# A PixArt block of 16 samples on one core: where the biases, the stacks and the maxima stand in hand-written plans

## The chip, the cores and the metric

The kernel runs on one core of a Trainium2 chip. The metric is the device time of one execution in microseconds; the median of three runs stands for the kernel. All times here are microseconds unless marked ns.

## The reference

16 samples, each with 256 tokens of 256 channels, all in fp32. For each sample, with `_ln` a layer norm without weights and 16 heads of 16 channels:

```
c_proj = silu(c) @ W_mod + b_mod       -> shift_a, scale_a, gate_a, shift_m, scale_m, gate_m
q, k, v = modulate(_ln(x), shift_a, scale_a) @ W_qkv + b_qkv
x = x + gate_a * (softmax(q k^T / 4) v @ W_proj + b_proj)            self attention
q_c = _ln(x) @ W_qc + b_qc;  k_c, v_c = _ln(context) @ W_kvc + b_kvc
x = x + softmax(q_c k_c^T / 4) v_c @ W_cproj + b_cproj               cross attention
x = x + gate_m * (gelu(modulate(_ln(x), shift_m, scale_m) @ W_mlp1 + b_mlp1) @ W_mlp2 + b_mlp2)
```

## The kernel before, in words

Names ending in x belong to self attention, in y to cross attention, m to the MLP, c to the context. Everything stays on the chip between stages of a sample; five engines each run one in-order program, tied by semaphores.

The work is a software pipeline over t from -1 to 18. Each t has a section A and a section B, each of 16 slots. In a slot of A, TensorE computes one head's scores of x(t) with queries on the partitions (the "scan", L637), of which VectorE takes the row maximum (L924), and one head's transposed scores of y(t-2) (L647), which ScalarE turns into P by an exponential (L778). In B the same is done with scans of y(t-1) and scores of x(t). There are two scan banks and two score banks in PSUM: slot s needs the reduction and the exponential of slot s-2.

Precision comes from splitting each fp32 operand into a high and a low part that TensorE takes at its rounded format. A query stack QS holds, per head pair and parity, 16 rows of high, 16 of high, 16 of low parts, and one row with the negated row maxima; a key stack KS holds high, low, high, and ones. ScalarE writes the high part of a projection (`projected`, L723, then semaphore `s_hi`), VectorE the low part (L840, then `s_lo`), and SyncE moves them into the stack with six transfers (L305), or for the queries of y, whose stack has only one buffer, six for each half (`q_y0`, `q_y1`, L317). The maxima are transposed on TensorE (L560), copied by ScalarE into MT (L751), and SyncE moves them into the stack's extra rows (`maxima`, L325): two transfers, one for each parity. TensorE waits for the stack before the first scan of a section, and for the maxima rows before slots 0 and 8 of the scores.

All other work is put between slots by plans: for each engine and section a list of (task, shift of t, slot), run in that order after the slot's own work (`run`, L270). SyncE and GpSimd have no slot work, so only the order counts for them. The tasks that matter here: `T_y` transposes the normed xn_y; `q_y` projects it; `norm_y` writes xn_y on VectorE (L825) with the inverse root of `root_y` from GpSimd (L397, L399); `x_bias`, `x1_bias` and `x2_bias` add a bias row to a residual on GpSimd (L441, L449, L458); `gate` multiplies the output weights by the gate (L434); `up0` to `up3`, `down0` and `down1` are the MLP; `pv_*` weights the values; `pt`, `pn`, `po` turn, norm and turn back its result. Projections and transposes go through two further PSUM banks in turn; a task waits until the one two places before it has been copied out (`take`, L511).

Of the kernel before, what the change touches and what calls it, by code (L numbers as in the profile page):

```python
# [4 lines left out]
fp32 = mybir.dt.float32  # L5
# [5 lines left out]
B, N, H, NH, MLP = 16, 256, 256, 16, 1024  # L11
HD = H // NH
# [11 lines left out]


SP_PLAN = {
    "A": [("gate_a", 0, 3), ("max_y1", -2, 3), ("gate_m", -3, 4), ("x_in", 2, 7), ("k_x", 1, 11), ("max_x0", 0, 12),
          ("q_y0", -1, 12), ("q_y1", -1, 13), ("q_x", 1, 15)],
    "B": [("c_in", 1, 0), ("max_x1", 0, 0), ("max_y0", -1, 1), ("k_y", 0, 4), ("out", -3, 15)],
}  # L30
PE_PLAN = {
    "A": [("up0a", -3, 0), ("up1a", -3, 0), ("up0b", -3, 0), ("up1b", -3, 0), ("pv_x3", -1, 1), ("max_y1", -2, 1),
          ("v_xa", 0, 2), ("v_xb", 0, 2), ("T_x", 1, 2), ("up2a", -3, 3), ("up2b", -3, 5), ("out_xa", -1, 5),
          ("out_xb", -1, 5), ("k_xa", 1, 7), ("k_xb", 1, 7), ("up3a", -3, 7), ("pv_y0", -2, 7), ("up3b", -3, 7),
          ("T_y", -1, 8), ("max_x0", 0, 9), ("pv_y1", -2, 9), ("q_ya", -1, 10), ("q_yb", -1, 10), ("q_xa", 1, 11),
          ("q_xb", 1, 12), ("pv_y2", -2, 15)],
    "B": [("pv_y3", -2, 1), ("max_x1", 0, 1), ("v_ya", -1, 1), ("v_yb", -1, 1), ("down0a", -3, 2), ("down0b", -3, 4),
          ("out_ya", -2, 4), ("out_yb", -2, 4), ("T_c", 0, 5), ("pv_x0", 0, 6), ("k_ya", 0, 7), ("k_yb", 0, 7),
          ("max_y0", -1, 9), ("pv_x1", 0, 9), ("T_m", -2, 11), ("down1a", -3, 11), ("down1b", -3, 13),
          ("pv_x2", 0, 15)],  # L40
}
ACT_PLAN = {
    "A": [("up0", -3, 0), ("up1", -3, 0), ("max_y1", -2, 1), ("v_x", 0, 2), ("T_x", 1, 2), ("up2", -3, 5),
          ("k_x", 1, 6), ("up3", -3, 7), ("T_y", -1, 7), ("q_y", -1, 10), ("max_x0", 0, 10), ("q_x", 1, 11)],
    "B": [("max_x1", 0, 0), ("v_y", -1, 0), ("T_c", 0, 5), ("k_y", 0, 7), ("max_y0", -1, 8), ("T_m", -2, 11)],
}
DVE_PLAN = {
    "A": [("pt_x1", -1, 0), ("stats_c", 0, 2), ("pn_x1", -1, 3), ("po_x1", -1, 3), ("out_x", -1, 5),
          ("stats_y", -1, 6), ("k_x", 1, 7), ("norm_y", -1, 7), ("T_y", -1, 8), ("pt_y0", -2, 10), ("q_y", -1, 11),
# [3 lines left out]
          ("stats_x", 2, 14)],  # L53
}
POOL_PLAN = {
    "A": [("norm_x", 1, 0), ("gate", -1, 2), ("T_x", 1, 3), ("root_y", -1, 7), ("x_bias", 0, 9), ("x2_bias", -3, 10)],
    "B": [("norm_c", 0, 0), ("norm_m", -2, 9), ("T_m", -2, 9), ("sum0", -3, 15), ("x1_bias", -1, 15),
          ("sum1", -3, 15)],
}
BANKED = {"up0", "up1", "up2", "up3", "max_x0", "max_x1", "max_y0", "max_y1", "out_x", "out_y", "T_c", "T_y", "T_x",  # L60
          "T_m", "k_x", "q_x", "k_y", "q_y", "v_x", "v_y", "down0", "down1"}
# [40 lines left out]
def build(nc, x, ctx_in, cond, bias, rows_in, bv_rows, wm1, wm2, wqk, wvx, wqc, wkvc, wo, wup, wdown, out):  # L102
# [3 lines left out]
    def wait(eng, sem, value):  # L106
        if value > 0:
            eng.wait_ge(sem, value)

    es = ExitStack()  # L110
    with es:
# [11 lines left out]
        def weight(start, blocks, cols):  # L123
# [12 lines left out]
        QS = {"x": [sb(f"QS_x{i}", [128, PAIRS, N], f32r) for i in range(2)],  # L136
              "y": [sb("QS_y", [128, PAIRS, N], f32r)] * 2}
# [24 lines left out]
        MT = [sb(f"MT{i}", [PAIRS, N], f32r) for i in range(2)]  # L162
# [9 lines left out]
        gate_a = sb("gate_a", [128, 2, H])  # L172
        gate_m = sb("gate_m", [128, 2, H])
# [43 lines left out]
        s_load = {k: sem(f"s_load_{k}") for k in ("q_x", "k_x", "q_y0", "q_y1", "k_y")}  # L217
        s_row = {s: [sem(f"s_row_{s}{i}") for i in range(2)] for s in "xy"}
# [62 lines left out]
        def _(sp):  # L281
# [208 lines left out]
        def _(pe):  # L490
# [186 lines left out]
        def _(act):  # L677
# [364 lines left out]
```

## Time and profile before

| | us |
|---|---|
| median of 3 runs | 1062.56 (1058.76 to 1063.86) |
| profiled execution, its own time | 1061.03 |
| its span, first to last instruction | 1059.2 |
| TensorE matmul busy | 931.7 (88%) |
| VectorE busy | 641.7 (61%) |
| ScalarE busy | 590.2 (56%) |
| GpSimd busy | 349.7 (33%) |
| mean granted TensorE clock | 0.911 of full |

The page's times are of one execution. Matmuls are pipelined, so their busy time is no measure of TensorE's peak; what counts here is where TensorE stands still, and who released it. A releaser "issue" is none of the instructions that the profile shows.

### The profile page before, as it was taken

What the parts mean: (1) busy time and instruction counts of PE and PEld (TensorE: products, weight loads), DVE (VectorE), ACT (ScalarE), POOL (GpSimd) and SP (SyncE); (2) the same over time, 40 slices, a digit from 0 to 9 for tenths busy, and PEclk for the clock granted to TensorE, in tenths of its full rate; (3) what the DMA queues carried; (4) which work ended last, traced back from release to release, by engine and by line L of the source; (5) the groups of instructions that cost most, each with busy time, mean ns of one, the idle gap of its engine ahead of it and who ended that gap; (6) DMA issues with size and microseconds to landing.
All of it is one profiled execution on the core that took longest, in us unless ns stands there. A gap on an engine that the chain in (4) does not pass through costs nothing.

```text
span 1059.2 us, 19372 instructions
## 1 busy us (share of the span) xinstructions
PE 931.7 (88%) x7216; PEld 678.6 (64%) x7216; DVE 641.7 (61%) x1302; ACT 590.2 (56%) x1058; POOL 349.7 (33%) x398
## 2 busy tenths in 40 slices
PE   5587889899898989899998989898999989797877
PEld 4446556667676757676676757576676767475646
DVE  3436567667675766666675767667675767553420
ACT  2151445748484756757474756657484757465252
POOL 4423042425051524334160525243251503230212
PEclk9567688999898989999899989899998999898888
DMA  7673535344335344353345362353433353021000
GB/s 202 147 92 58 92 59 93 65 88 81 72 62 110 62 89 63 84 88 64 71 84 86 62 105 63 81 75 73 85 75 71 72 91 62 32 43 38 11 11 30
DMA packets 77695, 79.21 MB, mean 75 GB/s; under 512 B 10113, under 2 KB 72194, under 8 KB 77218
## 3 DMA queue, kind: packets, MB, share of 16 engines
q1 hardware_dynamic: 77314, 77.44, 38.6%
q8 instruction: 58, 0.95, 0.4%
q10 hardware_dynamic: 288, 0.54, 0.2%
q14 instruction: 35, 0.29, 0.1%
HBM read 22.82 MB, written 4.26 MB: 26 GB/s over the span
## 4 chain that ended last, share of the span: by engine, by line
PE 73%; ACT 8%; DVE 7%; issue 6%; DMA 2%; SPq 1%; POOL 1%; ACTq 0%; POOLq 0%; DVEq 0%
PE bank L541 17%; PE scan L637 12%; PE pv L593 11%; PE bank L580 10%; PE score L647 6%; PE bank L551 6%; PE bank L571 5%; PE bank L522 4%; DVE xn_y L825 3%; ACT P L778 2%; ACT L778 2%; PE bank L560 2%; ACT SK L723 1%; DVE SK L840 1%; SPq L305 1%
## 5 line engine op out<-in xcount | busy, mean ns | idle before, releaser
L778 ACT ACTIVATE P<-score 128x512 f32<-128x512 f32 x512 | 289.4, 594 | 193.5 <-PE score L647 188.7
L924 DVE TENSOR_REDUCE MX_y<-scan 128x2 fp32r<-128x512 f32 x256 | 169.2, 681 | 92.4 <-PE scan L637 92.1
L924 DVE TENSOR_REDUCE MX_x<-scan 128x2 fp32r<-128x512 f32 x256 | 171.3, 681 | 71.8 <-PE scan L637 71.8
L647 PE MATMUL score<-QS_y,KS_y 49*128 49x256 f32 x512 | 122.2, 334 | 26.1 <-ACT P L778 25.9
L637 PE MATMUL scan<-KS_x,QS_x 48*128 48x256 f32 x512 | 127.7, 349 | 18.3 <-DMA QS_x<-SQ_x 9.8
L541 PE MATMUL bank<-xT_y,W 128*128 128x256 f32 x960 | 141.0, 295 | 0.5 <-ACT HH L731 0.5
L397 POOL TENSOR_TENSOR var_eps_m<-mv_m,eps 128x2 f32<-128x2 f32 x16 | 3.1, 196 | 413.6 <-DVE mv_m L818 413.6
L637 PE MATMUL scan<-KS_y,QS_y 48*128 48x256 f32 x512 | 113.1, 335 | 30.1 <-issue 22.1
L541 PEld LDWEIGHTS bank<-xT_y,W 128*128 128x128 f32 x960 | 123.1, 194 | 16.3 <-issue 7.5
L637 PEld LDWEIGHTS scan<-KS_y,QS_y 48*128 48x128 f32 x512 | 77.6, 205 | 81.9 <-issue 64.2
L580 PE MATMUL bank<-w_down,HH 128*128 128x256 f32 x512 | 128.9, 398 | 1.0 <-ACT HH L731 1.0
L637 PEld LDWEIGHTS scan<-KS_x,QS_x 48*128 48x128 f32 x512 | 79.4, 200 | 63.0 <-issue 36.5
L647 PE MATMUL score<-QS_x,KS_x 49*128 49x256 f32 x512 | 114.8, 339 | 2.3 <-DMA QS_x<-MT 1.1
L580 PEld LDWEIGHTS bank<-w_down,HH 128*128 128x128 f32 x512 | 95.5, 196 | 18.6 <-ACT HH L731 1.2
L647 PEld LDWEIGHTS score<-QS_y,KS_y 49*128 49x128 f32 x512 | 74.8, 191 | 38.3 <-ACT P L778 34.6
L848 DVE STREAM_TRANSPOSE PT<-pv 128x512 f32<-128x512 f32 x64 | 45.5, 712 | 79.6 <-PE pv L593 79.6
L593 PE MATMUL pv<-P,V_y 128*32 128x256 f32 x1024 | 88.3, 475 | 0.0
L647 PEld LDWEIGHTS score<-QS_x,KS_x 49*128 49x128 f32 x512 | 78.0, 206 | 7.1 <-ACT P L778 4.7
L541 PE MATMUL bank<-xT_x,W 128*128 128x256 f32 x384 | 62.9, 312 | 14.3 <-ACT MT L751 11.1
L593 PE MATMUL pv<-P,V_x 128*32 128x256 f32 x1024 | 73.0, 405 | 0.0
L541 PEld LDWEIGHTS bank<-xT_x,W 128*128 128x128 f32 x384 | 53.2, 207 | 22.2 <-ACT MT L751 14.1
L731 ACT ACTIVATE HH<-bank,bias_cols 128x256 f32<-128x256 f32 x128 | 51.9, 471 | 14.0 <-PE bank L541 13.7
(109 smaller groups left out, 1384.6 us busy)
## 6 DMA issues: line engine op xcount, KB each, us to landing
KS_x<-SK SPq DMA_DIRECT2D x96, 128.0 KB, 4.5
QS_x<-SQ_x SPq DMA_DIRECT2D x96, 128.0 KB, 4.6
KS_y<-SK SPq DMA_DIRECT2D x96, 128.0 KB, 4.5
QS_y<-SQ_y SPq DMA_DIRECT2D x192, 64.0 KB, 2.6
x_in<-in_x SPq DMA_DIRECT2D x16, 256.0 KB, 3.3
c_in<-in_ctx SPq DMA_DIRECT2D x16, 256.0 KB, 5.1
gate_a<-d_gate SPq DMA_DIRECT2D x16, 256.0 KB, 3.2
gate_m<-d_gate SPq DMA_DIRECT2D x16, 256.0 KB, 3.4
```

The costliest lines, as they stand in the source:

```text
L522: last = nc.tensor.transpose(to[:, c * N + a * 128:c * N + (a + 1) * 128], xn[k][:, a, c * 128:(c + 1) * 128], ident[:, :])
L541: last = nc.tensor.matmul(to[:, i * N:(i + 1) * N], w[p][:, c, (blk + i) * 128:(blk + i + 1) * 128], xT[k][:, q, c, :], start=(n == 0), st ...
L551: last = nc.tensor.matmul(to[:, a * H:(a + 1) * H], xT[k][:, p, c, a * 128:(a + 1) * 128], w[q][:, c, c0:c0 + H], start=(n == 0), stop=(n ...
L571: last = nc.tensor.matmul(to[:, a * H:(a + 1) * H], OT[:, half, a * 128:(a + 1) * 128], w[:, half, :], start=(half == 0), stop=(half == 1))
L580: last = nc.tensor.matmul(to[:, 0:H], HH[:, c, a * 128:(a + 1) * 128], w_down[:, c, :], start=(c == 0), stop=(c == FB - 1))
L593: last = nc.tensor.matmul(pv_bank[half % NPV][32 * j:32 * j + 32, g * N:(g + 1) * N], V[s][:, kb, head_of(half, g, j), :], P[:, (4 * grp + ...
L637: scanned = nc.tensor.matmul(scan_bank[n % NSCAN][:, i * N:(i + 1) * N], QS[s1][b1 % 2][row:row + 3 * HD, p, i * 128:(i + 1) * 128], KS[s1 ...
L647: scored = nc.tensor.matmul(score_bank[s % 2][:, i * N:(i + 1) * N], KS[s2][b2 % 2][row:row + 3 * HD + 1, p, i * 128:(i + 1) * 128], QS[s2 ...
L731: last = nc.scalar.activation(HH[:, 2 * u + i, :], src[:, i * N:(i + 1) * N], ACT.Gelu_apprx_tanh, bias=bias_cols[:, col:col + 1])
L778: nc.scalar.activation(P[:, s % 8, :, :].rearrange("p a n -> p (a n)"), score_bank[s % 2][:, :], ACT.Exp, scale=SCALE).then_inc(s_exp, 1)
L848: nc.vector.transpose(PT[:, :, :, :].rearrange("p a b c -> p (a b c)"), pv_bank[half % NPV][:, :])\
L924: nc.vector.tensor_reduce(MX[s1][:, half, :, par, p], scan_bank[n % NSCAN][:, :].rearrange("p (a n) -> p a n", a=NB), AXIS.X, ALU.max, neg ...
```

## The change

- `stack`: SyncE waits for `s_hi`, sends the four transfers of high parts, waits for `s_lo`, sends the two of low parts. `half_stack` does the same for its first half.
- `maxima`: one transfer writes both rows (partitions 48 and 112) in place of two; the counts that TensorE and ScalarE wait for are halved to match.
- GpSimd: `gate` stands before `norm_x`; `x2_bias` and `x_bias` before `root_y` instead of behind it; `sum0` before `norm_m`, and `x1_bias` last.
- All five plans have other slots and in part another order.

```diff
 SP_PLAN
-    "A": [("gate_a", 0, 3), ("max_y1", -2, 3), ("gate_m", -3, 4), ("x_in", 2, 7), ("k_x", 1, 11), ("max_x0", 0, 12),
-          ("q_y0", -1, 12), ("q_y1", -1, 13), ("q_x", 1, 15)],
-    "B": [("c_in", 1, 0), ("max_x1", 0, 0), ("max_y0", -1, 1), ("k_y", 0, 4), ("out", -3, 15)],
+    "A": [("gate_a", 0, 1), ("gate_m", -3, 4), ("max_y1", -2, 8), ("x_in", 2, 9), ("k_x", 1, 10), ("q_y0", -1, 12),
+          ("max_x0", 0, 13), ("q_x", 1, 15), ("q_y1", -1, 15)],
+    "B": [("max_x1", 0, 0), ("c_in", 1, 1), ("max_y0", -1, 4), ("k_y", 0, 4), ("out", -3, 4)],
 PE_PLAN
-          ("v_xa", 0, 2), ("v_xb", 0, 2), ("T_x", 1, 2), ("up2a", -3, 3), ("up2b", -3, 5), ("out_xa", -1, 5),
-          ("out_xb", -1, 5), ("k_xa", 1, 7), ("k_xb", 1, 7), ("up3a", -3, 7), ("pv_y0", -2, 7), ("up3b", -3, 7),
-          ("T_y", -1, 8), ("max_x0", 0, 9), ("pv_y1", -2, 9), ("q_ya", -1, 10), ("q_yb", -1, 10), ("q_xa", 1, 11),
-          ("q_xb", 1, 12), ("pv_y2", -2, 15)],
-    "B": [("pv_y3", -2, 1), ("max_x1", 0, 1), ("v_ya", -1, 1), ("v_yb", -1, 1), ("down0a", -3, 2), ("down0b", -3, 4),
-          ("out_ya", -2, 4), ("out_yb", -2, 4), ("T_c", 0, 5), ("pv_x0", 0, 6), ("k_ya", 0, 7), ("k_yb", 0, 7),
-          ("max_y0", -1, 9), ("pv_x1", 0, 9), ("T_m", -2, 11), ("down1a", -3, 11), ("down1b", -3, 13),
-          ("pv_x2", 0, 15)],
+          ("v_xa", 0, 2), ("v_xb", 0, 2), ("T_x", 1, 3), ("up2a", -3, 3), ("up2b", -3, 5), ("out_xa", -1, 5),
+          ("out_xb", -1, 5), ("k_xa", 1, 7), ("k_xb", 1, 7), ("up3a", -3, 7), ("up3b", -3, 7), ("pv_y0", -2, 7),
+          ("T_y", -1, 8), ("max_x0", 0, 9), ("pv_y1", -2, 9), ("q_ya", -1, 9), ("q_yb", -1, 9), ("q_xa", 1, 12),
+          ("q_xb", 1, 13), ("pv_y2", -2, 14)],
+    "B": [("pv_y3", -2, 0), ("max_x1", 0, 0), ("v_ya", -1, 1), ("v_yb", -1, 1), ("down0a", -3, 1), ("down0b", -3, 3),
+          ("T_c", 0, 3), ("out_ya", -2, 5), ("out_yb", -2, 5), ("pv_x0", 0, 5), ("k_ya", 0, 7), ("k_yb", 0, 7),
+          ("max_y0", -1, 8), ("pv_x1", 0, 8), ("T_m", -2, 10), ("down1a", -3, 12), ("down1b", -3, 14),
+          ("pv_x2", 0, 14)],
 ACT_PLAN
-          ("k_x", 1, 6), ("up3", -3, 7), ("T_y", -1, 7), ("q_y", -1, 10), ("max_x0", 0, 10), ("q_x", 1, 11)],
-    "B": [("max_x1", 0, 0), ("v_y", -1, 0), ("T_c", 0, 5), ("k_y", 0, 7), ("max_y0", -1, 8), ("T_m", -2, 11)],
+          ("k_x", 1, 6), ("up3", -3, 7), ("T_y", -1, 7), ("q_y", -1, 9), ("max_x0", 0, 9), ("q_x", 1, 13)],
+    "B": [("max_x1", 0, 0), ("v_y", -1, 2), ("T_c", 0, 3), ("k_y", 0, 7), ("max_y0", -1, 8), ("T_m", -2, 12)],
 DVE_PLAN
-    "A": [("pt_x1", -1, 0), ("stats_c", 0, 2), ("pn_x1", -1, 3), ("po_x1", -1, 3), ("out_x", -1, 5),
-          ("stats_y", -1, 6), ("k_x", 1, 7), ("norm_y", -1, 7), ("T_y", -1, 8), ("pt_y0", -2, 10), ("q_y", -1, 11),
-          ("q_x", 1, 13), ("pn_y0", -2, 14), ("po_y0", -2, 15)],
-    "B": [("pt_y1", -2, 0), ("pn_y1", -2, 0), ("po_y1", -2, 0), ("down0", -3, 3), ("out_y", -2, 4), ("T_c", 0, 5),
-          ("stats_m", -2, 5), ("k_y", 0, 9), ("pt_x0", 0, 10), ("down1", -3, 13), ("pn_x0", 0, 14), ("po_x0", 0, 14),
-          ("stats_x", 2, 14)],
+    "A": [("pt_x1", -1, 0), ("pn_x1", -1, 1), ("po_x1", -1, 3), ("stats_c", 0, 4), ("out_x", -1, 5),
+          ("stats_y", -1, 5), ("norm_y", -1, 7), ("k_x", 1, 7), ("T_y", -1, 8), ("pt_y0", -2, 8), ("q_y", -1, 10),
+          ("pn_y0", -2, 15), ("q_x", 1, 15), ("po_y0", -2, 15)],
+    "B": [("pt_y1", -2, 1), ("pn_y1", -2, 1), ("po_y1", -2, 3), ("down0", -3, 3), ("T_c", 0, 4), ("out_y", -2, 5),
+          ("stats_m", -2, 5), ("k_y", 0, 8), ("pt_x0", 0, 10), ("pn_x0", 0, 12), ("down1", -3, 13),
+          ("stats_x", 2, 15), ("po_x0", 0, 15)],
 POOL_PLAN
-    "A": [("norm_x", 1, 0), ("gate", -1, 2), ("T_x", 1, 3), ("root_y", -1, 7), ("x_bias", 0, 9), ("x2_bias", -3, 10)],
-    "B": [("norm_c", 0, 0), ("norm_m", -2, 9), ("T_m", -2, 9), ("sum0", -3, 15), ("x1_bias", -1, 15),
-          ("sum1", -3, 15)],
+    "A": [("gate", -1, 0), ("norm_x", 1, 3), ("T_x", 1, 4), ("x2_bias", -3, 4), ("x_bias", 0, 5), ("root_y", -1, 15)],
+    "B": [("norm_c", 0, 0), ("sum0", -3, 6), ("norm_m", -2, 6), ("T_m", -2, 10), ("sum1", -3, 11),
+          ("x1_bias", -1, 13)],
 def stack(which, s, b)
-                sp.wait_ge(s_lo[f"{which}_{s}"], b + 1)
+                sp.wait_ge(s_hi[f"{which}_{s}"], b + 1)
...
-                for par in range(2):
-                    for c, part in enumerate(parts):
+                for part in (HI, LO):
+                    if part == LO:
+                        sp.wait_ge(s_lo[f"{which}_{s}"], b + 1)
+                    for c in (c for c in range(3) if parts[c] == part):
+                        for par in range(2):
...
 def maxima(s, half, b)
-                for par in range(2):
-                    row = 64 * par + 3 * HD
-                    sp.dma_start(QS[s][b % 2][row:row + 1, 4 * half:4 * half + 4, :].bitcast(fp32),
-                                 MT[half][4 * par:4 * par + 4, :].bitcast(fp32)).then_inc(s_row[s][half], 16)
+                sp.dma_start(QS[s][b % 2][3 * HD:3 * HD + 65:64, 4 * half:4 * half + 4, :].bitcast(fp32),
+                             MT[half][:, :].bitcast(fp32)).then_inc(s_row[s][half], 16)
```

## Rows read from the trace of the kernel before

**Rows 1.** Windows: us, busy and count of PE, PEld, DVE, ACT, POOL, then PEclk, DMA share, GB/s

```profile
182.95:884.53 701.58, 648.33 (x5380) 476.78 (x5377) 474.48 (x960) 440.98 (x792) 254.79 (x290) 0.96 0.43 78
474.66:507.46 32.80, 28.11 (x248) 21.28 (x245) 23.33 (x49) 24.61 (x42) 13.33 (x15) 1.00 0.34 74
507.46:534.27 26.81, 26.81 (x204) 19.34 (x204) 16.27 (x32) 12.11 (x24) 7.82 (x9) 0.88 0.51 79
...
860.63:884.53 23.90, 23.90 (x204) 17.37 (x205) 16.18 (x32) 12.11 (x24) 7.94 (x10) 1.00 0.59 89
943.87:972.79 28.92, 21.95 (x174) 15.11 (x171) 9.72 (x21) 21.29 (x34) 3.47 (x4) 0.92 0.14 40
```

**Rows 2.** Waits of TensorE over the span: total us, times, longest

```profile
PE score L647 <- ACT P L778: 26.9, 37, 1.7
PE scan L637 <- issue: 22.1, 15, 3.7
PE bank L522 <- DVE xn_y L825: 16.6, 16, 2.2
PE bank L541 <- ACT MT L751: 11.1, 14, 0.8
```

**Rows 3.** Timeline of TensorE, end of one section A: start, duration, instruction, idle before

```profile
493.50 0.66 PE L522 MATMUL bank<-ident,xn_y 128*128 128x128 f32 x4 [0.83 <-DVE xn_y L825]
...
494.82 1.07 PE L593 MATMUL pv<-P,V_y 128*32 128x256 f32 x16
...
496.81 0.38 PE L647 MATMUL score<-QS_y,KS_y 49*128 49x256 f32 x1 [0.60 <-ACT P L778]
...
497.24 1.68 PE L541 MATMUL bank<-xT_y,W 128*128 128x256 f32 x12
...
507.46 0.55 PE L637 MATMUL scan<-KS_y,QS_y 48*128 48x256 f32 x1 [1.51 <-issue]
```

**Rows 4.** Timeline of SyncE's transfers in the same section

```profile
500.14 1.32 SPq L325 DMA_DIRECT2D QS_x<-MT  x2
501.57 7.63 SPq L317 DMA_DIRECT2D QS_y<-SQ_y  x12
```

**Rows 5.** The page's queues (packets, MB, share) and issues (count, KB, us to landing)

```profile
q1 hardware_dynamic: 77314, 77.44, 38.6%
...
QS_y<-SQ_y SPq DMA_DIRECT2D x192, 64.0 KB, 2.6
...
c_in<-in_ctx SPq DMA_DIRECT2D x16, 256.0 KB, 5.1
```

**Rows 6.** Timeline of VectorE in the same section

```profile
487.45 0.69 DVE L876 TENSOR_TENSOR x<-bank,x_bias 128x512 f32<-128x512 f32 x1 [1.12 <-PE bank L571]
...
488.66 0.74 DVE L814 BATCH_NORM_STATS2 stats_y<-x 128x6 f32<-128x256 f32 x2
489.44 0.25 DVE L818 BATCH_NORM_AGGREGATE mv_y<-stats_y 128x2 f32<-128x6 f32 x2
...
491.44 2.00 DVE L825 TENSOR_SCALAR xn_y<-x,mv_y,rstd_y 128x256 f32<-128x256 f32 x2
...
499.99 0.87 DVE L840 SCALAR_TENSOR_TENSOR SQ_y<-bank,bias_cols,SQ_y 128x256 fp32r<-128x256 f32 x2
```

**Rows 7.** Timeline of GpSimd in the same section

```profile
490.04 0.71 POOL L399 TENSOR_TENSOR rstd_y<-var_eps_y,minus_half 128x2 f32<-128x2 f32 x1
490.72 1.29 POOL L441 TENSOR_TENSOR x_bias<-x_in,gate_a 128x512 f32<-128x512 f32 x1
491.96 1.32 POOL L458 TENSOR_TENSOR x_bias<-x,gate_m 128x512 f32<-128x512 f32 x1
```

**Rows 8.** Timeline of VectorE in the section of t=1, the same norm

```profile
93.44 0.73 DVE L825 TENSOR_SCALAR xn_y<-x,mv_y,rstd_y 128x256 f32<-128x256 f32 x2
```

**Rows 9.** Timeline of ScalarE in the section of rows 3

```profile
494.86 1.28 ACT L778 ACT_TABLE_LOAD   x1
...
499.04 0.84 ACT L723 ACTIVATE SQ_y<-bank,bias_cols 128x256 fp32r<-128x256 f32 x2 [1.10 <-PE bank L541]
```

More of the change, by code:

```diff
@@ L41 @@
 }
 ACT_PLAN = {
-    "A": [("up0", -3, 0), ("up1", -3, 0), ("max_y1", -2, 1), ("v_x", 0, 2), ("T_x", 1, 2), ("up2", -3, 5),
-          ("k_x", 1, 6), ("up3", -3, 7), ("T_y", -1, 7), ("q_y", -1, 10), ("max_x0", 0, 10), ("q_x", 1, 11)],
-    "B": [("max_x1", 0, 0), ("v_y", -1, 0), ("T_c", 0, 5), ("k_y", 0, 7), ("max_y0", -1, 8), ("T_m", -2, 11)],
+    "A": [("up0", -3, 0), ("up1", -3, 0), ("max_y1", -2, 2), ("v_x", 0, 2), ("T_x", 1, 3), ("up2", -3, 5),
+          ("k_x", 1, 6), ("up3", -3, 7), ("T_y", -1, 7), ("q_y", -1, 9), ("max_x0", 0, 9), ("q_x", 1, 13)],
@@ L298, in stack @@
                 src, dst, parts = {"q": (SQ[s], QS[s][b % 2], (HI, HI, LO)), "k": (SK, KS[s][b % 2], (HI, LO, HI))}[which]
-                sp.wait_ge(s_lo[f"{which}_{s}"], b + 1)
+                sp.wait_ge(s_hi[f"{which}_{s}"], b + 1)
                 if b >= 2:
                     sp.wait_ge(s_score_full, SCORES[s, b - 2] + NH)
-                for par in range(2):
-                    for c, part in enumerate(parts):
-                        row = 64 * par + HD * c
-                        sp.dma_start(dst[row:row + HD, :, :].bitcast(fp32),
-                                     src[:, part, par, :].bitcast(fp32)).then_inc(s_load[f"{which}_{s}"], 16)
+                for part in (HI, LO):
[3 more added lines that the diff above has]
+                        for par in range(2):
+                            row = 64 * par + HD * c
+                            sp.dma_start(dst[row:row + HD, :, :].bitcast(fp32),
+                                         src[:, part, par, :].bitcast(fp32)).then_inc(s_load[f"{which}_{s}"], 16)
             def half_stack(half, b):
                 if half == 0:
-                    sp.wait_ge(s_lo["q_y"], b + 1)
+                    sp.wait_ge(s_hi["q_y"], b + 1)
                 if b >= 1:
                     sp.wait_ge(s_score_full, SCORES["y", b - 1] + PAIRS * (half + 1))
-                for par in range(2):
-                    for c, part in enumerate((HI, HI, LO)):
+                for c, part in enumerate((HI, HI, LO)):
+                    if half == 0 and part == LO:
+                        sp.wait_ge(s_lo["q_y"], b + 1)
+                    for par in range(2):
                         row = 64 * par + HD * c
@@ L322, in maxima @@
                 sp.wait_ge(s_MT[s][half], b + 1)
-                for par in range(2):
-                    row = 64 * par + 3 * HD
-                    sp.dma_start(QS[s][b % 2][row:row + 1, 4 * half:4 * half + 4, :].bitcast(fp32),
-                                 MT[half][4 * par:4 * par + 4, :].bitcast(fp32)).then_inc(s_row[s][half], 16)
+                sp.dma_start(QS[s][b % 2][3 * HD:3 * HD + 65:64, 4 * half:4 * half + 4, :].bitcast(fp32),
+                             MT[half][:, :].bitcast(fp32)).then_inc(s_row[s][half], 16)
             def load_gate_a(b):
@@ L630, in slot @@
                     if scores is not None and s % PAIRS == 0:
-                        pe.wait_ge(s_row[s2][s // PAIRS], 32 * (b2 + 1))
+                        pe.wait_ge(s_row[s2][s // PAIRS], 16 * (b2 + 1))
                     for i in range(NB):
@@ L746, in maxima @@
                 if s == "x":
-                    wait(act, s_row["y"][half], 32 * (b - 1))
+                    wait(act, s_row["y"][half], 16 * (b - 1))
                 else:
-                    act.wait_ge(s_row["x"][half], 32 * min(b + 2, B))
+                    act.wait_ge(s_row["x"][half], 16 * min(b + 2, B))
                 src = full(act, f"max_{s}{half}", b)
```

## The prediction

> **What bounds the kernel now.** I read the windows first, then TensorE's waits, then one period in order of time on each engine. Between 182.95 and 884.53 us the kernel runs 12 equal periods, so one takes 701.58/12 = 58.47 us, and TensorE is busy in 648.33 of the 701.58 [rows 1]. A period is a section A and a section B. A (474.66 to 507.46) takes 32.80 us with 28.11 us of matmuls at the full clock. B has no idle time at all, but it takes 26.81 us at a granted clock of 0.88 in one period and 23.90 us at 1.00 in another [rows 1]. So a period at full clock would be 32.80 + 23.90 = 56.70 us, and 58.47 - 56.70 = 1.77 us a period (21 us over the twelve) is lost to clock: the half level, 1.2 GHz, granted for a few us behind the border from A to B.
>
> A's 4.69 us of idle time are what a new order can win. The waits name them, nearly one of each per period: matmuls of scores behind exponentials (26.9 us), transposes behind xn_y (16.6 us), the projection behind MT (11.1 us), and "issue" in front of the first scan of B (22.1 us) [rows 2]. The same places in one period are at 493.50 (0.83), 496.81 (0.60) and 507.46 (1.51) [rows 3]. They are one chain: xn_y, its transposes T_y, ScalarE's copy, VectorE's low part, the projection q_y, its high and low parts, SyncE's transfers, B. "Issue" is no engine's doing: SyncE issues the two maxima at 500.14, then twelve QS_y transfers from 501.57 in 7.63 us, 0.636 each [rows 4]. The sixth, the last that B's first slot needs, is issued at 501.57 + 5 x 0.636 = 504.75, and with 2.6 us to landing [rows 5] it lands at 507.35; B starts at 507.46. A lasts as long as this chain, whatever the matmuls do.
>
> **The change, part by part** (times from A's start, 474.66 = 0).
>
> *Biases on GpSimd.* xn_y takes 2.00 us for two instructions in slot 7, while x_bias (490.72, 1.29 us) and x2_bias (491.96, 1.32 us) run on GpSimd [rows 6, 7]. In an early period without x2_bias, and x_bias elsewhere, the same pair takes 0.73 us [rows 8]. So beside the biases 1.27 us are lost, for 16 times. In the new order x2_bias and x_bias stand before root_y. x2_bias needs only old results and runs in GpSimd's gap before 13 us. x_bias(t) waits for x1 of t-1, that is until out_x ends at 488.14 = 13.5, and takes 1.29: until 14.8. It now delays root_y: out_x, then stats_y at once (slot 5, no scan between: 0.69 + 0.74 + 0.25 and gaps) gives the mean and variance at 14.5; root_y starts at 14.8 instead, a loss of 0.3, and takes about 1.0 (its second instruction, at 490.04, is 0.71). The row before has the inverse root at 490.75 = 16.1 [rows 7]; new 15.8. xn_y now precedes k_x's low part, and ends at 15.9 + 0.8 = 16.7 against 18.8. T_y may start when slot 8's matmuls are done, at 493.50 - 0.83 - 474.66 = 18.0. The stall of 0.83 goes, with 1.3 us to spare. norm_c follows root_y on GpSimd, and its own root covers xn_y. k_x's low part comes 0.8 later for nobody: its stack is read a section and more later.
>
> The Trainium skill, "SBUF — State Buffer", section "SBUF: two separate sides", says that VectorE and GpSimd share one port pair, held for a whole instruction against a VectorE instruction in a two-port mode or with two SBUF inputs. By that rule x_bias beside stats_y (one input) costs nothing, and moving the biases recovers the full difference; the trace's 0.73 against 2.00 agrees, but does not show the lock.
>
> *Order around q_y.* Before, slot 10 stands between pv_y1 and q_y and waits 0.60 for an exponential, because ScalarE reloads its table (494.86, 1.28) [rows 3, 9]. Now q_y is in slot 9. From T_y's start to pv_y1's end the old rows take 494.82 + 1.07 - 493.50 = 2.4 at most (the next matmul overlaps its tail) [rows 3], so q_y starts at 20.3 instead of 22.6. ScalarE starts its high part 1.80 after q_y's start (499.04 against 497.24 [rows 3, 9]): 22.1, ready at 22.95. Slots 10 and 11 need exponentials 8 and 9, which end about 21.3 and 21.9 with the table load 0.8 earlier: no wait. Slot 12 needs exponential 10, which is queued on ScalarE behind q_y and the MT copy: 22.95 + 0.3 + 0.6 = 23.8, TensorE is there at 22.9. This is a stall of 0.9, in place of the old 0.60, 0.82 and 0.92. q_x moves behind it, so MT is no longer waited for. TensorE ends A at about 28.4.
>
> *High parts on their own.* SyncE now starts with s_hi, not s_lo. Old: it starts q_y0 at 501.57 = 26.9: low part ready at 26.2 (499.99 + 0.87, [rows 6]), then the rest of the maxima pair. New: four high transfers from 23.0, the low part is ready at 24.0 and so never waited for, six issued by 23.0 + 3.8 = 26.8. Last landing 26.2 + 2.6 = 28.8. For k_x, k_y and q_x the gain of 0.9 is hidden, since their stacks have half a period. The added wait between high and low of q_x (VectorE's low part is now in slot 15, behind reduction and pn_y0, ready near 30.8) holds SyncE from 30.2 to 30.8; behind it are q_y1 and max_x1, needed in B's slot 8, near 44: hidden.
>
> *Maxima in one transfer, behind q_y0.* 1.32 us of issue become one of 0.66 [rows 4], and it no longer stands in front of q_y0. It is issued at 26.9. Nothing in the trace gives its landing: below, no later than the stack (28.8); above, like a 64 KB one, 26.9 + 2.6 = 29.5. I take 29.4, near the row. So B starts at 29.4 instead of 32.8: 3.4 us less. The other three maxima of a period are needed 4 us and more after issue: hidden.
>
> The Trainium skill, "DMA: Bandwidth & Descriptors", section "Why a DMA increments its semaphore by 16 and not by 1", has a rule against this edit: a transfer is spread over as many engines as divides both slowest dimensions. The old ones have 4 and 4, the new one 2 (rows of QS) and 8, so two engines carry four 1 KB pieces each. From the queue's row, 38.6% of 16 x 1059.2 us over 77314 packets is 0.085 us a packet [rows 5]; three more in line are 0.25 us, which would put B at 29.7 and the whole 4 us later. No row here shows the spread.
>
> *Section B.* down0, out_y and T_m are set about one slot apart from before, all matmuls are the same. I look at its two tight places. stats_m follows out_y directly; out_y to xn_m is 0.13 + 0.69 + 1.03 + 1.0 + 2.5, about 5.6 us, against 6.1 us of matmuls until T_m: 0.5 spare. sum0 and sum1 go to where GpSimd idles; gate ahead of norm_x delays it by 1.3, T_x is one slot later, 1.6 spare. down1 on VectorE waits for slot 14's matmuls with reduction 14 behind it: 0.2 spare before A's first scan. So B stays 23.90 at full clock; I bound the three together by 0 and +0.7 and take 0.
>
> *Sum.* Against the profiled execution, 1061.0 us (span 1059.2, 1.8 around it): 13 full sections A at 3.4 = 44.2; three with part of their work, such as 943.87 to 972.79 with 28.92 us [rows 1], at 2.0 = 6; the first stacks 1.0 earlier = 1. Fewer and shorter idle stretches in A should leave some of the half-level stretches out; which, no row tells. I take a quarter of the 21 us, 5, ends -5 (more of them) and 21. Together 56: 1004.8. The median of the runs is 1.5 above the profiled one: 1006.
>
> **Rivals.** (1) *The chain is cut only once.* VectorE or ScalarE is late around slots 9 to 12 (pt_y0 is now in front of reduction 9, both maxima and q_y in one slot), so only the 0.83 and the 0.9 of the high parts arrive, 1.7 a section: 16 x 1.7 = 27, 1035. For it: ScalarE is busy for 24.61 of A's 32.80, in a 29.4 us A that is 84%. Against: each hand-over above is a measured interval. (2) *The clock comes back wholly*: another 16 us off, 990. For it: B at 23.90 exists [rows 1]; against, it exists with the same stalls. (3) *Slower: the single transfer lands late.* Place: B's first slot and, half a period later, A's. Price: B starts at 26.9 plus its landing time, so it decides from 32.8 - 26.9 = 5.9 us on. c_in's landing of 5.1 [rows 5] is the slowest steady one; at 8 us it would be +2.1 for 16 sections, 1096. Against: it is 4 KB. (4) *Given back in B*: xn_m misses T_m by the whole gain; it would have to be 3.9 us late, nothing in the rows is: no change, 1062.
>
> **How the numbers follow.** My forecast 0.66, rival 1 0.17, rival 2 0.07, rival 3 0.05, rival 4 0.05. The forecast's own range is 994 to 1020; with rival 2 at its edge and rival 1 inside, 989 to 1037. Within 0.5% (5 us, about what can be told from no change): rival 4, 0.05. Slower: rival 3 and a share for an unseen queue, 0.06. Faster: 0.89.
>
> **What would show it.** After: A near 29.4 and B near 24 at full clock; xn_y's pair near 0.75; no wait for xn_y or MT in TensorE's waits; one wait for an exponential near slot 12 of 0.9; the first scan of B waits about 1 us. QS_y's first issue 3.9 us earlier in A. Wrong if A stays above 31, if TensorE waits in B, or if reductions, not transfers, end the waits.

## The result, and the profile after

The changed kernel takes 980.58 us (977.0 to 982.67, 4 runs) against 1062.62 (1058.76 to 1063.86, 4 runs) of the kernel before: ratio 0.923, 95% interval [0.9194, 0.9266]. The forecast was 1006 with a range down to 989, so the direction held and the size did not: 82 us instead of 56, outside the range. In the profiled executions the span went from 1059.2 to 980.9. Executions of one kernel differ in how long TensorE was granted only half its clock: the profiled ones of b_order (1065.28) and a_pool (1037.07), used below, have a mean clock of 0.886 against 0.904 to 0.922 in these kernels' other executions, and lie well above their medians.

The windows of the changed kernel, columns as in rows 1: until the first full period, the 12 full periods, the rest, then one section A and one B that meet no half-level clock (1.2 GHz):

```profile
0.00:166.04 166.04, 126.67 (x874) 90.06 (x875) 97.13 (x206) 64.52 (x125) 54.45 (x66) 0.83 0.59 117
166.04:811.73 645.69, 626.83 (x5378) 462.23 (x5378) 455.39 (x960) 442.27 (x792) 254.44 (x290) 0.98 0.47 84
811.73:980.90 169.17, 144.00 (x970) 105.12 (x966) 65.43 (x136) 83.74 (x141) 39.30 (x44) 0.86 0.12 31
705.72:734.36 28.64, 27.14 (x248) 20.70 (x245) 20.10 (x44) 25.24 (x43) 14.42 (x16) 1.00 0.36 80
734.36:758.73 24.37, 24.27 (x205) 17.39 (x206) 17.88 (x37) 11.64 (x23) 6.76 (x9) 1.00 0.69 93
```

And the kernel before, for the two stretches that rows 1 do not have:

```profile
0.00:182.95 182.95, 139.42 (x874) 97.21 (x874) 98.67 (x207) 66.06 (x126) 56.98 (x67) 0.77 0.54 106
...
884.53:1059.20 174.67, 143.99 (x970) 104.64 (x966) 68.57 (x137) 83.14 (x140) 37.98 (x43) 0.87 0.11 30
```

So 55.9 of the 78.3 us of span are won in the 12 periods (701.58 to 645.69), 16.9 before them, 5.5 behind them. A section A without half level went from 32.80 to 28.64, a section B from 23.90 to 24.37. TensorE's waits in the changed kernel, to be set beside [rows 2]:

```profile
PE scan L640 <- DVE MX_x L927: 18.6, 25, 3.7
PE scan L640 <- DMA QS_x<-SQ_x: 9.1, 1, 9.1
PE scan L640 <- DMA QS_y<-SQ_y: 8.0, 8, 2.9
PE score L650 <- ACT P L781: 7.7, 9, 2.4
...
PE bank L525 <- DVE xn_y L828: 1.7, 3, 1.0
```

The waits for xn_y fell from 16.6 to 1.7 and none of them is in the 12 periods, the wait for MT (11.1) is gone, and the waits for exponentials fell from 26.9 to 7.7. Two places of a period are left: 0.55 before slot 12's scan, and 0.3 to 1.4 before B. The chain of one section A, which starts at 705.72, in the changed kernel's timelines (compare [rows 3, 4, 6, 7, 9]), first TensorE's:

```profile
723.16 0.66 PE L525 MATMUL bank<-ident,xn_y 128*128 128x128 f32 x4
...
725.50 1.70 PE L544 MATMUL bank<-xT_y,W 128*128 128x256 f32 x12
...
728.41 0.38 PE L640 MATMUL scan<-KS_x,QS_x 48*128 48x256 f32 x1 [0.55 <-DVE MX_x L927]
...
734.36 0.35 PE L640 MATMUL scan<-KS_y,QS_y 48*128 48x256 f32 x1 [0.82 <-DVE MX_x L927]
```

The same place one period earlier, at the end of the A that starts at 653.20, and the VectorE instruction that the last row above names:

```profile
681.35 0.35 PE L640 MATMUL scan<-KS_y,QS_y 48*128 48x256 f32 x1 [0.34 <-DMA QS_y<-SQ_y]
```

```profile
733.58 0.69 DVE L927 TENSOR_REDUCE MX_x<-scan 128x2 fp32r<-128x512 f32 x1 [0.74 <-PE scan L640]
```

SyncE's queue in the section from 705.72:

```profile
728.18 4.22 SPq L322 DMA_DIRECT2D QS_y<-SQ_y  x6
732.45 0.55 SPq L328 DMA_DIRECT2D QS_x<-MT  x1
```

For ScalarE, the eviction of q_y:

```profile
727.32 0.84 ACT L726 ACTIVATE SQ_y<-bank,bias_cols 128x256 fp32r<-128x256 f32 x2 [0.36 <-PE bank L544]
```

For VectorE, the norm:

```profile
721.34 0.74 DVE L828 TENSOR_SCALAR xn_y<-x,mv_y,rstd_y 128x256 f32<-128x256 f32 x2 [0.20 <-POOL rstd_y L402]
```

And for GpSimd:

```profile
719.06 1.29 POOL L444 TENSOR_TENSOR x_bias<-x_in,gate_a 128x512 f32<-128x512 f32 x1 [0.63 <-DVE x L879]
...
720.59 0.71 POOL L402 TENSOR_TENSOR rstd_y<-var_eps_y,minus_half 128x2 f32<-128x2 f32 x1
```

The reader finds the forecast's steps here: xn_y takes 0.74, T_y starts at 17.4 of the section without a wait (forecast 18.0), q_y at 19.8 (20.3), SyncE at 22.5 (23.0), the maxima go out at 26.73 (26.9), B starts 1.91 later at 28.64 (29.4).

The prediction called itself wrong if reductions, not transfers, ended the waits, and the row at 734.36 names a reduction. It is not what held B. The reduction that ends at 734.27 is that of slot 15, and B's first scan needs the bank of slot 14; one period earlier B waits 0.34 and the profile names the transfer. In the trace B starts at least 0.09 behind the last landing of its stack (here 734.19) and at least 1.91 behind the issue of the maxima. By these two numbers the maxima decide in 7 of the 12 periods, but only by about 0.1. The time from the first to the sixth transfer of the stack varies: each is issued 0.59 to 0.65 after the one before, but in 6 of the 12 periods one takes 1.1 to 1.7. In this section it is the third (1.12). Without such a gap and with a stack landing after 2.4, as in the A that starts at 653.20, A takes 28.15. The kernel before has no such gap in these periods. What causes them is open.

### The profile page after: what moved, and what is told of

Read it like the earlier page. It is cut to its first block, busy times and chain, and to the rows that moved or that the text cites. A ratio compares the mean times of both kernels' runs of the same rounds, so it can differ in the third digit from the quotient of the medians.

```text
span 980.9 us, 19308 instructions
## 1 busy us (share of the span) xinstructions
PE 897.5 (91%) x7216; PEld 657.4 (67%) x7216; DVE 617.9 (63%) x1302; ACT 590.5 (60%) x1058; POOL 348.2 (35%) x398
## 4 chain that ended last, share of the span: by engine, by line
PE 76%; DVE 6%; ACT 4%; DMA 4%; SPq 4%; issue 4%; POOL 2%; POOLq 0%; ACTq 0%; DVEq 0%
PE bank L544 18%; PE scan L640 14%; PE pv L596 12%; PE bank L583 11%; PE bank L554 6%; PE bank L574 5%; PE score L650 4%; PE bank L525 3%; SPq L322 3%; DVE MX_y L927 2%; PE bank L563 2%; DMA QS_y<-SQ_y 2%; ACT P L781 2%; DVE MX_x L927 1%; DMA QS_x<-SQ_x 1%
## 5 line engine op out<-in xcount | busy, mean ns | idle before, releaser
L640 PE MATMUL scan<-KS_x,QS_x 48*128 48x256 f32 x512 | 121.4, 336 | 25.8 <-DVE MX_x L927 16.2
L467 POOL TENSOR_TENSOR y<-y,x_bias 128x256 f32<-128x256 f32 x32 | 23.3, 728 | 329.7 <-DVE y L895 329.7
L544 PE MATMUL bank<-xT_y,W 128*128 128x256 f32 x960 | 136.1, 292 | 2.3 <-DVE xT_y L835 1.7
L640 PE MATMUL scan<-KS_y,QS_y 48*128 48x256 f32 x512 | 111.3, 327 | 19.8 <-DMA QS_y<-SQ_y 8.0
L650 PE MATMUL score<-QS_y,KS_y 49*128 49x256 f32 x512 | 116.8, 330 | 8.1 <-ACT P L781 6.3
L640 PEld LDWEIGHTS scan<-KS_x,QS_x 48*128 48x128 f32 x512 | 76.6, 196 | 68.9 <-issue 30.3
L640 PEld LDWEIGHTS scan<-KS_y,QS_y 48*128 48x128 f32 x512 | 74.0, 195 | 69.8 <-issue 54.7
L650 PE MATMUL score<-QS_x,KS_x 49*128 49x256 f32 x512 | 111.7, 328 | 1.5 <-ACT P L781 1.5
L596 PE MATMUL pv<-P,V_y 128*32 128x256 f32 x1024 | 77.1, 424 | 1.5 <-ACT P L781 1.5
L650 PEld LDWEIGHTS score<-QS_x,KS_x 49*128 49x128 f32 x512 | 73.8, 195 | 5.3 <-ACT P L781 4.1
```

Source lines behind the costliest of these rows:

```text
L544: last = nc.tensor.matmul(to[:, i * N:(i + 1) * N], w[p][:, c, (blk + i) * 128:(blk + i + 1) * 128], xT[k][:, q, c, :], start=(n == 0), st ...
L596: last = nc.tensor.matmul(pv_bank[half % NPV][32 * j:32 * j + 32, g * N:(g + 1) * N], V[s][:, kb, head_of(half, g, j), :], P[:, (4 * grp + ...
L640: scanned = nc.tensor.matmul(scan_bank[n % NSCAN][:, i * N:(i + 1) * N], QS[s1][b1 % 2][row:row + 3 * HD, p, i * 128:(i + 1) * 128], KS[s1 ...
L650: scored = nc.tensor.matmul(score_bank[s % 2][:, i * N:(i + 1) * N], KS[s2][b2 % 2][row:row + 3 * HD + 1, p, i * 128:(i + 1) * 128], QS[s2 ...
```

## The experiments

Each was timed beside the kernel before on the same chip, and ratios are to that. The last columns are of the profiled execution: time before the first full period, the 12 periods, and the half-level stretches that begin in them, summed from the trace's record of the granted clock. after2 is the changed kernel once more and a_s12b is a_s12 once more, on another chip.

```
kernel       median   ratio [95%]             start  12 periods  half level
before       1062.6   1                       182.9  701.6       58
changed      980.6    0.923  [0.919, 0.927]   166.0  645.7       24
b_hi         1059.2   0.998  [0.995, 1.001]   178.1  703.2       61
b_pool       1047.6   0.987  [0.984, 0.991]   181.7  690.5       68
b_order      1049.4   0.988  [0.984, 0.993]   181.2  705.7       96
b_fill       1050.9   0.991  [0.987, 0.994]   184.8  690.7       24
a_lo         1001.1   0.944  [0.941, 0.948]   175.3  654.1       20
a_two        997.5    0.939  [0.935, 0.944]   171.9  652.5       27
a_pool       1022.5   0.962  [0.957, 0.968]   172.7  689.8      106
a_pool_kx    1006.0   0.946  [0.939, 0.953]   173.0  667.2       61
a_pool_fill  1023.6   0.965  [0.959, 0.971]   171.0  671.9       55
a_pool_s12   1001.7   0.943  [0.939, 0.948]   166.7  658.1        7
a_busy       1000.9   0.940  [0.937, 0.944]   172.7  657.5       14
a_fill       978.2    0.919  [0.912, 0.926]   169.4  639.3        7
a_start      979.9    0.925  [0.922, 0.929]   166.1  642.2       17
a_both       985.0    0.927  [0.921, 0.932]   166.6  649.5       27
a_s12        975.3    0.917  [0.916, 0.919]   167.6  639.2        0
after2       980.1    0.924  [0.920, 0.927]   169.4  640.5       14
a_s12b       975.6    0.919  [0.917, 0.922]   165.9  638.3        0
```

**Parts alone in the kernel before.** b_hi has the new `stack` and `half_stack` (its first line is below; the loops go by part, as in the change), b_pool the new POOL_PLAN, b_order the other four plans (in ScalarE's, max_y1 also goes from slot 1 to 2 and T_x from 2 to 3, which the lines under "The change" leave out). The fourth part, one transfer of maxima in place of two, is in none of them:

```diff
-                sp.wait_ge(s_lo[f"{which}_{s}"], b + 1)
+                sp.wait_ge(s_hi[f"{which}_{s}"], b + 1)
...
```

> The kernel before with one part alone: the stacks' high parts on their own. My theory by its steps: in the steady sections the maxima pair is issued first and until 501.46, so the q_y0 stack still starts at 26.9 of a section; no gain there (0), 1 to 3 us from the first stacks: 1060. Rival, that the wait for the low part alone was worth 0.9 us of each of 16 sections: 1047.

> The kernel before with GpSimd's new order alone. Theory: the xn_y pair takes 0.75 us instead of 2.00, the wait of 0.83 before its transposes goes and the chain to section B comes 0.8 earlier, 16 times: 13 us, and where the shorter chain leaves fewer half-level clock stretches, up to 8 more: 1042 to 1050. Rival, that the chain does not carry the 0.83 on to section B (another wait takes it): 1060.

> The kernel before with the new plans of SyncE, TensorE, ScalarE and VectorE alone (GpSimd's order, the stacks' wait for the low part and the two maxima transfers as before). Theory: q_y in slot 9 brings it 2.2 us earlier; against the changed kernel SyncE starts 0.95 later (low part) and the second maxima transfer adds 0.6: section A near 30.3, 40 us of the gain, and about half of the clock's: 1005 to 1015. Rival, that the parts need each other and the order alone leaves section A at 32: 1045.

b_hi did what the first theory said: 1059.2, no measurable change, as the maxima pair stands in front of q_y0. b_pool is in its band's upper half, 1047.6. b_order missed, by 34 to 44 us: 1049.4. Its waits tell why:

```profile
PE scan L637 <- DMA QS_x<-MT: 26.0, 13, 3.4
PE bank L522 <- DVE SK L840: 17.1, 12, 1.4
```

The new order without the new GpSimd order makes T_y wait 1.42 in each period, now for the low part of k_x, and the maxima pair, still two transfers and now behind q_y0, holds B for 2.0. By their ratios the three parts alone add to 29 us. All four together bring 82, and what the fourth would bring alone was not run; undone in the changed kernel it costs 17 (a_two, below).

**Parts undone in the changed kernel.** a_lo has the old `stack` and `half_stack`, a_two the two transfers of maxima, a_pool the old POOL_PLAN.

```diff
-    "A": [("gate", -1, 0), ("norm_x", 1, 3), ("T_x", 1, 4), ("x2_bias", -3, 4), ("x_bias", 0, 5), ("root_y", -1, 15)],
+    "A": [("norm_x", 1, 0), ("gate", -1, 2), ("T_x", 1, 3), ("root_y", -1, 7), ("x_bias", 0, 9), ("x2_bias", -3, 10)],
```

> The changed kernel with one part undone: SyncE again waits for the low part before it sends any of a stack. Theory: the q_y0 stack starts 0.95 later in each of 16 sections, all of it on the chain: 15 us and some clock, 996 to 1003. Rival, that reductions of VectorE end the wait at the border (as the waits after name them) and hide it: 981 to 985.

> The changed kernel with two maxima transfers, as before. Theory: one issue more, 0.55 us, in front of the last landing of each of 16 sections, but that landing is spread over more engines: 5 to 9 us, 986 to 990. Rival, that the landing does not bind: 981.

> The changed kernel with GpSimd's old order. Theory: xn_y runs beside the biases again, 2.0 us, but now starts at 15.3 of the section, before k_x's low part, and ends near 17.3 where slot 8's matmuls end at 17.4: hidden, 981 to 985. Rival, that the biases cost as much as in the kernel before, 0.8 in 16 sections: 994.

a_lo came at 1001.1, in its band, with 20.6 us lost. a_two missed its band: 997.5, with 16.9 lost where 5 to 9 were expected. In the 12 periods they lose 8.4 and 6.8, that is 0.70 a period where 0.95 was expected and 0.57 where 0.55 was; in sections without a long gap between transfers A takes 29.14 and 28.91 against 28.15. Another 9.3 and 5.9 are lost before the first full period, which a_two's expectation left out, and 2.8 and 2.0 behind the last. The start alone scatters by 3 us between two executions of the changed kernel (166.0 and 169.4). That a_lo's B comes a us later also shows that it is the transfers that B waits for. a_pool missed: 1022.5, 42 us lost, where none was expected. VectorE in the timeline of one of its periods (A starts at 340.31):

```profile
355.66 2.65 DVE L828 TENSOR_SCALAR xn_y<-x,mv_y,rstd_y 128x256 f32<-128x256 f32 x2
358.23 0.86 DVE L843 SCALAR_TENSOR_TENSOR SK<-bank,bias_cols,SK 128x256 fp32r<-128x256 f32 x2
```

GpSimd in the same timeline:

```profile
355.59 1.29 POOL L444 TENSOR_TENSOR x_bias<-x_in,gate_a 128x512 f32<-128x512 f32 x1
356.83 1.33 POOL L461 TENSOR_TENSOR x_bias<-x,gate_m 128x512 f32<-128x512 f32 x1
```

And TensorE:

```profile
359.24 0.63 PE L525 MATMUL bank<-ident,xn_y 128*128 128x128 f32 x4 [1.42 <-DVE SK L843]
364.46 0.38 PE L640 MATMUL scan<-KS_x,QS_x 48*128 48x256 f32 x1 [0.55 <-DVE MX_x L927]
```

xn_y starts just behind the first bias and lasts for both, 2.65 (1.29 + 1.33 = 2.62), against 0.74 alone. The Trainium skill, "SBUF — State Buffer", section "SBUF: two separate sides", says that the loser of the shared port pair is blocked for the whole instruction. The trace agrees: each of xn_y's two instructions, 0.41 alone, lasts 1.37 here and ends about 0.15 behind one addition. That it is this port pair and nothing else that they share, no run shows. What the expectation left out is behind it in the queue: k_x's low part empties the PSUM bank that T_y takes (k_x, up3, T_y with two banks). It ends at 359.09, and TensorE waits 1.42. And then the clock; windows of this period, cut at T_y, at slot 12 and 10.4 us later:

```profile
340.31:359.24 18.93, 17.51 (x158) 14.10 (x155) 14.63 (x32) 17.12 (x28) 11.34 (x14) 1.00 0.18 60
359.24:364.40 5.16, 4.67 (x46) 3.23 (x46) 3.13 (x6) 4.00 (x8) 2.43 (x2) 1.00 0.93 144
364.40:374.80 10.40, 9.91 (x66) 5.62 (x66) 6.27 (x14) 4.61 (x10) 0.00 (x0) 0.60 0.45 91
374.80:398.33 23.53, 23.44 (x183) 17.26 (x184) 15.77 (x32) 11.05 (x22) 7.40 (x9) 0.96 0.41 74
```

From 366.5 on, 2.1 behind slot 12's first scan, the half level, 1.2 GHz, is granted. Such a stretch of 10.2 us comes in ten of this execution's twelve periods, all but the first two, always at this place. These periods last 58.0; the second, which has no half level, lasts 54.0.

a_pool_kx swaps two tasks of DVE_PLAN on top of a_pool:

```diff
-           ("stats_y", -1, 5), ("norm_y", -1, 7), ("k_x", 1, 7), ("T_y", -1, 8), ("pt_y0", -2, 8), ("q_y", -1, 10),
+           ("stats_y", -1, 5), ("k_x", 1, 7), ("norm_y", -1, 7), ("T_y", -1, 8), ("pt_y0", -2, 8), ("q_y", -1, 10),
```

> GpSimd's old order in the changed kernel, and VectorE with k_x's low part ahead of norm_y, as in the kernel before. T_y needs the bank that k_x's low part empties, and now stands behind a norm that shares time with the biases. Theory: the bank is free by 16.5 of the section and T_y waits for xn_y alone, which ends near 17.8 to 18.4: 0.4 to 1.0 instead of 1.42, and with a shorter wait fewer half-level stretches, 990 to 1010. Rival, that the order on VectorE is indifferent: 1020 to 1025.

1006.0, in its band. T_y now waits 0.81 in each period, for xn_y:

```profile
PE bank L525 <- DVE xn_y L828: 15.8, 16, 2.0
```

Swapping two tasks on VectorE brings 17 of the 42 us back, more than the 0.6 of wait in 16 sections; the half level of the 12 periods fell with it, from 106 to 61 (in profiled executions that are both the longest of their kernel). That supports the queue behind the bank, since the wait for it is gone.

**Idle time filled with matmuls whose results nothing uses.** They multiply constant weights into a bank that is free by then and is overwritten; nothing else of the computation changes. b_fill has ten of them in front of each section B from t = 2 on; a_fill is the same with four in the changed kernel, a_start has sixty in one block at the start, a_both those sixty and six at the border:

```diff
+                if 2 <= t <= B:
+                    pe.wait_ge(s_exp, SCORES["y", t - 2] + NH - 1)
+                    fill(10)
```

> The kernel before with ten matmuls more (constant weights on constant weights, into a score bank that is free and is overwritten) at the end of each section A from t = 2 on, in TensorE's idle time in front of section B; nothing else changes. Theory that the half-level stretches (58 us of them between 182.95 and 884.53, worth 21 us) hang on that idle time: section A stays at 32.8, the stretches mostly go, 1040 to 1050. Rival, that they come whatever stands at the border: no faster, 1062 to 1066.

> The changed kernel with four matmuls more (0.44 us, results unused) in the idle time in front of section B, from t = 2 on. Theory that idle time at the border brings the half level: of the 24 us of half-level stretches between 166 and 812 most go, 972 to 978. Rival, that they come in any case: 981 to 986.

> The changed kernel and sixty matmuls more (6.6 us at full clock, results unused) in front of the first section A with scans, where TensorE waits 9 us for the first stack. Theory that this idle time brings the half level of the start (58 us of it before t = 3): 4 to 10 us off, 970 to 977. Rival, that the start's half level hangs on the thin sections after it: 979 to 982.

> The changed kernel with both fillings, sixty matmuls at the start and six at the end of each section A. Theory: what each brings adds up, 965 to 975, the fastest of all here. Rival, that filling costs what it brings: 978 to 984.

b_fill made the kernel before 11 us faster by giving it 150 matmuls more: 1050.9, 0.9 above its theory's band and 11 below its rival's. The half level in its 12 periods went from 58 us to 24, though the matmuls take nothing off the chain. Its window over the 12 periods:

```profile
184.82:875.50 690.68, 651.14 (x5502) 483.92 (x5498) 473.99 (x960) 441.38 (x792) 254.82 (x290) 0.98 0.43 79
```

In the changed kernel less is left: a_fill is at 978.2, between its two bands, and its interval covers the changed kernel's, so it decides nothing. a_start is a miss, 979.9: the half level before 166 us went from 58.0 to 47.8 us, and the time did not follow. a_both is one too, 985.0: with six matmuls instead of four at the border, eight stretches of 3.4 us come, all in section A behind slot 12 (27 us). TensorE's idle time in each section A is 0.7 to 1.0 here, against 1.0 to 2.2 in the changed kernel's without half level, and yet there are eight stretches in place of four. Less idle time does not in itself mean less half level.

Then, on a_pool, the wait before T_y filled (a_pool_fill), and slot 12's wait too (a_pool_s12); and on the changed kernel, busy matmuls where no wait is (a_busy), and slot 12 and the border filled (a_s12). The first block is that of a_pool_fill and a_pool_s12 (a_busy has 13 in place of 11), the second that of a_pool_s12 and a_s12:

```diff
+                if name == "T_y" and b >= 1:
+                    pe.wait_ge(s_exp, SCORES["y", b - 1] + 8)
+                    for _ in range(11):
+                        nc.tensor.matmul(score_bank[1][:, 0:N], W[:, HI, 0:128], W[:, HI, 0:N], start=True, stop=True)
...
+                    if letter == "A" and s == 12 and 2 <= t <= B - 1:
+                        pe.wait_ge(s_pt, half_index("y", t - 2, 1) - NPV + 1)
+                        for _ in range(5):
+                            nc.tensor.matmul(pv_bank[1][:, 0:N], W[:, HI, 0:128], W[:, HI, 0:N], start=True, stop=True)
```

> GpSimd's old order in the changed kernel, as in the run before it, and eleven matmuls more (1.2 us, results unused) in TensorE's idle time in front of the transposes T_y, from t = 2 on. There the wait of 1.42 us before T_y is followed in each period by 10.2 us of half-level clock. Theory that the clock answers to that idle time: the wait's own 17 us stay, nearly all half-level stretches go, 995 to 1003. Rival, that GpSimd's order costs its 41 us in another way: 1020 to 1025.

> GpSimd's old order in the changed kernel, with TensorE's wait before T_y filled (eleven matmuls) and the wait of 0.55 us before slot 12 too (five, into a value bank that is free). Theory that the wait in slot 12, where every stretch of half level begins, brings it: the stretches go, 998 to 1006. Rival, that they come whether or not it is filled: 1015 to 1028.

> The changed kernel and thirteen matmuls more (1.43 us, results unused) in front of T_y from t = 2 on, where it has no idle time: each section A becomes longer and later by about 1.4 us, all of it busy. Theory that idle time brings the half level: only the matmuls' own 15 x 1.4 = 21 us, 1000 to 1003. Rival, that a section longer by that much meets the half level in any case, as in the runs with GpSimd's old order: 1015 to 1028.

> The changed kernel with four matmuls more at the end of section A and five before slot 12, both in idle time. Theory that little idle time is left to bring the half level: 968 to 976, the fastest here. Rival, that the filling is not hidden or the half level comes anyway: 978 to 985.

The first fell: 1023.6, nothing gained with T_y's wait filled. The second held: 1001.7, with 0.55 us a period more filled, 22 us came back. The window over the 12 periods, of a_pool_fill:

```profile
170.97:842.89 671.92, 656.99 (x5511) 485.75 (x5510) 477.10 (x960) 441.84 (x792) 254.49 (x289) 0.96 0.44 81
```

Of a_pool_s12:

```profile
166.66:824.80 658.14, 645.59 (x5572) 482.85 (x5570) 477.30 (x960) 442.47 (x792) 255.17 (x290) 0.99 0.46 83
```

Of a_busy:

```profile
172.71:830.20 657.49, 641.63 (x5536) 479.31 (x5534) 455.05 (x960) 442.29 (x792) 253.47 (x289) 0.99 0.46 83
```

a_pool_s12 and a_busy have the same section length, one by a filled wait, the other by work, and the same time, 1001.7 and 1000.9: 20 to 21 us above the changed kernel, which is the 1.4 us of 15 sections and no more. So of a_pool's 42 us some 21 are the wait, and some 21 come with the half level and go with it. Length alone does not bring the half level, and in a_pool_fill filling the wait in slot 12 ends it. But that wait alone does not bring it either. For TensorE a_busy and a_pool_fill are nearly the same: sections A without half level take 29.6 to 30.6, with 0.55 idle in slot 12, 0.3 to 1.2 at the border and no other wait above 0.15. Yet the one has 14 us of half level and the other 55, and they take 1000.9 and 1023.6. In a_pool_fill and a_pool a stretch of 10.2 us is mostly followed by another in the next period. Whether the exact time of the matmuls matters, rather than their idle time alone, was not tested, and which idle time the half level follows is open.

a_s12 is the fastest kernel here, 975.3, with no half level in its 12 periods:

```profile
167.58:806.80 639.22, 633.25 (x5486) 471.40 (x5486) 455.56 (x960) 442.51 (x792) 253.51 (x289) 1.00 0.49 85
```

It was timed again beside the changed kernel on one chip, six executions each:

> The changed kernel again, on the same chip as the next: 978 to 983 by both theories.

> Nine matmuls more in the idle time of each section A, again. Theory: 4 to 8 us below the changed kernel on this chip, 973 to 977. Rival, that the first comparison was the chip's: within 2 us of it.

980.12 for the changed kernel, ratio 0.9239 [0.9204, 0.9273], and 975.55, ratio 0.9193 [0.9165, 0.9221], for the filled one. Both comparisons give 5 us, 0.5%; here the intervals overlap a little, so it is likely, not certain.

## Why the prediction was wrong in size

*The chain* was right, link for link but for slot 12 (below): xn_y 0.74 (forecast 0.75), no wait for it or for MT, q_y in slot 9, the transfers from 22.5, B about a us behind TensorE's last matmul. A section lost 4.16 instead of 3.4. The term of the section that was mis-sized is the landing of the single transfer: B starts 1.91 behind its issue, not 2.5; I took the upper bound, the row of 64 KB. (It carries 8 KB, not the 4 KB that rival 3 gives it.) The other 0.2: SyncE starts 0.5 earlier than forecast, and the long gap in this section takes most of that back. Over 12 periods the term was 9 us short. Rival 3, a late landing, is refuted by the same 1.91, and rival 1 by the section itself. By the rule on spreading of the Trainium skill, "DMA: Bandwidth & Descriptors", section "Why a DMA increments its semaphore by 16 and not by 1", the prediction put B at 29.7. The runs show no such cost: in a_two, whose two transfers have the old shape, B starts 1.99 behind the issue of the second, no sooner than the 1.91 here. No run isolates the rule.

*Slot 12*: forecast a wait of 0.9 for an exponential; it is 0.55 for a reduction. ScalarE was 0.5 earlier throughout, and VectorE's reduction 10 ends last.

*Section B* was taken as unchanged; it is 24.37 against 23.90, 5.6 us lost over 12 periods. No wait explains it: the busy time of B rose by 0.37 and that of A fell by 0.97. In B's rows the scans and the scores rose, each from 6.4 to 6.7 for 32 matmuls, and the rest stayed within 0.1. Why is open.

*The clock is the step that failed*, in the 12 periods and most of all before them. I wrote "I take a quarter of the 21 us, 5". In the 12 periods, 55.9 won less 12 x 4.16 for A plus 12 x 0.47 for B leaves 11.6 us for the clock; half-level stretches went from 58 us to 24. And the start was not asked at all: I gave it 5 us (1 for the stacks, two thin sections at 2.0), and it won 16.9. Its mean clock went from 0.77 to 0.83, and 85 us of half level to 58. By the rows above TensorE's 874 matmuls there took 126.67 instead of 139.42, 12.7 less, and its idle time fell by 4.2 (43.5 to 39.4). So most of the 16.9 is a faster clock on the same matmuls, and 4.2 is idle time. That thin sections suffer more since they have the same chain and less work to cover it is my reading; the undone parts agree with it (a_lo loses 9.3 of its 20.6 there, with 75 us of half level against 58). The second profiled execution of the changed kernel, after2, has 169.4 there, so 3 us of the term are scatter. The term for the thin sections came from one row behind the periods, and what stands behind them came out as forecast: 5.4 (3.4 + 2.0) against 5.5. Errors of the terms against the 56: A +9, B -6, clock in the periods +7, start +12, together 22, and the profiled spans differ by 78.

Rival 2, the clock back wholly, was half right in the periods (11.6 of the 21) and had too low a chance, 0.07. Its 990 still lies above the 980.6 measured, because it too left the start out. The range should have reached further down for both.

*The biases* were credited with the 0.83 of T_y's wait only, 13 us. In the changed order they are worth 42, because the old order would now also delay the bank behind the norm (1.42 a period) and is followed by more half level (106 us against 24). The forecast for the whole did not suffer, since it walked the new order as a whole.

## What to carry to other kernels

Walk the chain of one period link by link with the trace's own intervals; here it came within 0.8 us of 28.6. Then price the clock by itself, with an upper end at all of the half level that the trace shows, and ask the start as well: here it had 85 us of it and the largest error. Parts of such a change can't be priced alone, since each only shows where the others have taken their waits away (three of the four bring 29 us alone, all four 82 together). A few idle-time matmuls are a cheap way to tell a wait's own cost from the clock's, but beside them a run is needed with the same length made of work: here it showed that idle time does not settle it alone.

## What the runs showed of the hardware

A kernel got faster by extra matmuls: 150 of them in idle time, 1062.1 to 1050.9 us. Idle times as short as 0.55 us were followed by 10.2 us at half level: in ten of twelve periods with another of 1.42 us in the same section (a_pool), in five with that one filled (a_pool_fill), in one in a_busy, where TensorE's idle times are nearly the same as in a_pool_fill. Filling the 0.55 ended it there (a_pool_s12). A VectorE norm of two instructions, 0.74 us, that starts just behind the start of GpSimd's two additions lasts for both, 2.65 us. A transfer of 8 KB between two places in SBUF could be used 1.91 us after its issue behind six of 64 KB.
